# Cross-attention: running maximum taken one step later, and 8 of 15 probability tiles multiplied as high and low parts

## The reference

```python
# latents [4, 256, 512], context [4, 1601, 512], 32 query heads, 8 key/value heads of 128
kv = jnp.concatenate([context, latents], axis=1)
q = rms_norm((latents @ Wq) in 32 heads, q_norm_w)
k = rms_norm((kv @ Wk) in 8 heads, k_norm_w)
v = (kv @ Wv) in 8 heads
scores = jnp.einsum('bhgqd,bhkd->bhgqk', qg, k) / sqrt(128)
probs = softmax(scores, axis=-1)
out = jnp.einsum('bhgqk,bhkd->bhgqd', probs, v)
return out.reshape(...) @ Wo
```

## Time and profile before

| | |
|---|---|
| median of 3 runs | 3105.89 us (3101.67 to 3109.8) |
| the profiled execution | 3108.48 us |
| its span in the trace | 3106.6 us |
| PE busy, from 340 to 2930 us | 2586.37 of 2590 us |
| POOL busy in the same stretch | 1559.72 us |

### The profile page before, as it was taken

How to read it: one execution, slowest core, us unless ns; L and a number is a source line. 1 busy time by engine, 2 the same in 40 slices (tenths; PEclk the granted TensorE clock), 3 DMA queues, 4 the chain that set the end, 5 groups by cost and what they waited for, 6 DMA issues and landing times. The chain is left out here.

```text
span 3106.6 us, 43885 instructions
## 1 busy us (share of the span) xinstructions
PE 2868.3 (92%) x14348; PEld 2136.8 (69%) x14348; DVE 2117.3 (68%) x3447; ACT 1776.2 (57%) x3228; POOL 1740.6 (56%) x1729
## 2 busy tenths in 40 slices
PE   2239999999999999999999999999999999999976
PEld 1127777777777777777777777777777777777644
DVE  6726677777777777777777777776776767676654
ACT  1015666666666666666666666666666666665541
POOL 4413556566565565656656556565665655655550
PEclk7659999999999999999999999999999999999985
DMA  0075343343433434334433433433433333333201
GB/s 34 27 243 191 116 134 127 125 140 127 134 124 127 138 123 136 125 127 138 136 120 129 140 126 123 136 122 128 143 114 108 125 109 104 114 109 103 68 7 65
DMA packets 155728, 370.12 MB, mean 119 GB/s; under 512 B 12777, under 2 KB 46571, under 8 KB 155504
## 3 DMA queue, kind: packets, MB, share of 16 engines
q1 hardware_dynamic: 153752, 365.49, 35.7%
q10 hardware_dynamic: 1752, 1.84, 0.2%
HBM read 329.53 MB, written 37.75 MB: 118 GB/s over the span
## 5 line engine op out<-in xcount | busy, mean ns | idle before, releaser
L664 POOL TENSOR_TENSOR acc<-acc,scores 128x512 f32<-128x512 f32 (+1 forms) x832 | 1068.2, 1284 | 652.0 <-ACT scores L915 628.5
L1078 DVE SCALAR_TENSOR_TENSOR running_max<-S_ps,rk,running_max 128x512 f32<-128x512 f32 (+1 forms) x896 | 672.2, 750 | 710.8 <-ACT scores L907 705.1
L915 ACT ACTIVATE scores<-scores 128x512 f32<-128x512 f32 (+1 forms) x960 | 605.0, 631 | 933.8 <-DVE scores L1062 933.3
L749 PE MATMUL OT_ps<-scores,V 128*128 128x512 f32 (+1 forms) x1920 | 987.6, 597 | 9.6 <-issue 3.0
L720 PE MATMUL S_ps<-QT_hi,KT_hi 128*128 128x512 f32 (+1 forms) x960 | 732.1, 763 | 9.4 <-DVE running_max L1078 6.8
L1062 DVE TENSOR_TENSOR scores<-scores,Mb_ps 128x512 f32<-128x512 f32 (+1 forms) x960 | 649.8, 678 | 35.3 <-PE Mb_ps L832 32.1
L907 ACT ACTIVATE scores<-S_ps,rk 128x512 f32<-128x512 f32 (+1 forms) x960 | 646.8, 674 | 22.6 <-PE S_ps L722 22.3
L720 PE MATMUL K_ps<-Wkv_hi,kvT 128*128 128x256 f32 (+1 forms) x1664 | 469.6, 282 | 1.7 <-DVE V L1111 1.0
L722 PE MATMUL K_ps<-Wkv_hi,kvT 128*128 128x256 f32 (+1 forms) x1664 | 470.0, 282 | 0.0
L721 PE MATMUL K_ps<-Wkv_lo,kvT 128*128 128x256 f32 (+1 forms) x1664 | 469.4, 282 | 0.0
L722 PE MATMUL S_ps<-QT_hi,KT_lo 128*128 128x512 f32 (+1 forms) x960 | 378.9, 395 | 0.0
(11 more groups left out here) (177 smaller groups left out, 3909.7 us busy)
## 6 DMA issues: line engine op xcount, KB each, us to landing
kvT<-kvT_scratch SPq DMA_DIRECT2D x416, 512.0 KB, 3.3
w_stage<-in_L_xattn_Wq SPq DMA_DIRECT2D x64, 512.0 KB, 4.4
w_stage<-in_L_xattn_Wo SPq DMA_DIRECT2D x64, 512.0 KB, 4.4
kvT_scratch<-built SPq DMA_DIRECT2D x60, 512.0 KB, 2.9
xrow<-in_ctx SPq DMA_DIRECT2D x48, 256.0 KB
w_stage<-in_L_xattn_Wk SPq DMA_DIRECT2D x32, 256.0 KB, 3.0
w_stage<-in_L_xattn_Wv SPq DMA_DIRECT2D x32, 256.0 KB, 3.3
xT<-kvT_scratch SPq DMA_DIRECT2D x8, 512.0 KB, 5.3
```

The costliest lines, as they stand in the source:

```text
L664: e.tensor_tensor(a[0:r, :], a[0:r, :], prob(t)[0:r, :], ALU.add).then_inc(s_acc, 1)
L749: ins = e.matmul(OT_ps[:], V[v % 2][0:r, j, :], row[t % RING][0:r, :], start=first, stop=last)
L915: e.activation(d, d, ACT.Exp).then_inc(s_p, 1)
L1078: e.scalar_tensor_tensor(a, src, k, a, ALU.mult, ALU.max).then_inc(s_top, 1)
```

## The change

A tile j in `HALF` = 0, 1, 4, 5, 8, 9, 12, 13 is now multiplied as high and low parts: ACT takes the exponential twice, once rounded to fp32r into `P_hi` and once in fp32 into `P_sb` (two buffers of each), POOL subtracts them into `P_lo` (two buffers), and PE makes three fp32r products with `V_hi` and `V_lo`. The values of these tiles are split by ACT (`V_hi`) and DVE (`V_lo`) where DVE copied them before. The other 7 tiles (`FULL`) go as before. `pv` of such a tile waits for `P_lo`. On DVE `raise_max` of step s moves behind `shift` of step s+1, and in step c = 5 job X comes ahead of MT.

```diff
-            5: [("MT", 2 * v - 2), ("X", b + 1, 2 * h)],
+            5: [("X", b + 1, 2 * h), ("MT", 2 * v - 2)],
...
+            def lo(t):
+                j = t % NJ
+                if j in FULL:
+                    return
+                r = rows_of(j)
+                n = half_no(t)
+                e.wait_ge(s_p, t + 1)
+                if n >= 2:
+
+                    e.wait_ge(s_pv, half_tile(n - 2) + 1)
+                e.tensor_tensor(P_lo[n % 2][0:r, :], P_sb[n % 2][0:r, :], f(P_hi[n % 2][0:r, :]), ALU.subtract)\
+                    .then_inc(s_lo, 1)
...
                 if 0 <= s - WAIT < NS:
+                    lo(s - WAIT)
                     add(s - WAIT)
...
-                e.wait_ge(s_p, t + 1)
-                ins = e.matmul(OT_ps[:], V[v % 2][0:r, j, :], row[t % RING][0:r, :], start=first, stop=last)
+                if j in FULL:
+                    e.wait_ge(s_p, t + 1)
+                    ins = e.matmul(OT_ps[:], V_full[v % 2][0:r, FULL.index(j), :], row[t % RING][0:r, :],
+                                   start=first, stop=last)
+                else:
+                    i, n = HALF.index(j), half_no(t)
+                    e.wait_ge(s_lo, n + 1)
+                    ins = three(OT_ps[:], V_hi[v % 2][0:r, i, :], V_lo[v % 2][0:r, i, :],
+                                P_hi[n % 2][0:r, :], P_lo[n % 2][0:r, :], first, last)
...
-                e.activation(d, d, ACT.Exp).then_inc(s_p, 1)
+                if j in HALF:
+                    n = half_no(t)
+                    if n >= 2:
+
+                        old = half_tile(n - 2)
+                        e.wait_ge(s_pv, old + 1)
+                        e.wait_ge(s_acc, acc_no(old + 1 if old % NJ == 0 else old))
+                    e.activation(P_hi[n % 2][0:r, :], d, ACT.Exp)
+                e.activation(prob(t)[0:r, :], d, ACT.Exp).then_inc(s_p, 1)
...
+                if q in HALF_PAIRS:
+                    i = HALF.index(js[0])
+                    if v >= 2:
+
+                        e.wait_ge(s_pv, NJ * (2 * v - 3) + js[-1] + 1)
+                    e.activation(V_hi[v % 2][0:r, i:i + k, :], src[0:r, 0:k, HD:2 * HD], ACT.Copy).then_inc(s_vh, 1)
...
+                if q in HALF_PAIRS:
+                    e.wait_ge(s_vh, half_pair_no(v, q) + 1)
+                    at = slice(HALF.index(js[0]), HALF.index(js[0]) + k)
+                    e.tensor_tensor(V_lo[v % 2][0:r, at, :], src[0:r, 0:k, HD:2 * HD], f(V_hi[v % 2][0:r, at, :]),
+                                    ALU.subtract).then_inc(s_kr, 1)
...
                 if 0 <= s - WAIT < NS:
                     shift(s - WAIT)
+                if 0 <= s - 1 < NS:
+                    raise_max(s - 1)
...
                 for v, q in pairs(s - 1):
-                    copy_values(v, q)
-                if 0 <= s < NS:
-                    raise_max(s)
+                    low_values(v, q)
```

More of the change, by code:

```diff
@@ L317, in cross_attention @@
     LAST = (UNITS + 2) * CYCLE - AHEAD
+    FULL = [2, 3, 6, 7, 10, 11, 14]
+    HALF = [j for j in range(NJ) if j not in FULL]
     EPS = 1e-6
@@ L417, in acc_no, with half_no, half_tile @@
         return (NJ - 1) * p + j
+    def half_no(t):
+        p, j = divmod(t, NJ)
+        return len(HALF) * p + HALF.index(j)
+    def half_tile(n):
+        p, i = divmod(n, len(HALF))
+        return NJ * p + HALF[i]
     with ExitStack() as ctx:
@@ L432, in cross_attention @@
         KT_lo = sb("KT_lo", [P, NKP], F32R)
-        V = [sb(f"V{i}", [P, NJ, HD]) for i in range(2)]
+        V_hi = [sb(f"V_hi{i}", [P, len(HALF), HD], F32R) for i in range(2)]
+        V_lo = [sb(f"V_lo{i}", [P, len(HALF), HD], F32R) for i in range(2)]
+        V_full = [sb(f"V_full{i}", [P, len(FULL), HD]) for i in range(2)]
         QT_hi = [sb(f"QT_hi{i}", [P, QW], F32R) for i in range(2)]
@@ L436, in cross_attention @@
         row = [sb(f"scores{i}", [P, QW]) for i in range(RING)]
+        P_sb = [sb(f"P32_{i}", [P, QW]) for i in range(2)]
+        P_hi = [sb(f"P_hi{i}", [P, QW], F32R) for i in range(2)]
+        P_lo = [sb(f"P_lo{i}", [P, QW], F32R) for i in range(2)]
         Wkv_hi = [sb(f"Wkv_hi{i}", [P, C, 2 * HD], F32R) for i in range(2)]
@@ L491, in cross_attention @@
         s_p = sem("probabilities")
+        s_lo = sem("probabilities_lo")
         s_acc = sem("probabilities_added")
@@ L506, in cross_attention @@
         s_kc = sem("K_rows_copied")
+        s_vh = sem("V_hi_copied")
         s_sq = sem("squares")
@@ L523, in prob, with half_pair_no @@
         def prob(t):
-            return row[t % RING]
+            return row[t % RING] if t % NJ in FULL else P_sb[half_no(t) % 2]
+        FULL_PAIRS = [q for q in range(8) if 2 * q in FULL]
+        HALF_PAIRS = [q for q in range(8) if 2 * q in HALF]
+        def half_pair_no(v, q):
+            return len(HALF_PAIRS) * v + HALF_PAIRS.index(q)
         @block.sync
@@ L904, in copy_scores @@
                     t = s - RING
-                    e.wait_ge(s_pv, t + 1)
-                    e.wait_ge(s_acc, acc_no(t + 1 if t % NJ == 0 else t))
+                    if t % NJ in HALF:
+                        e.wait_ge(s_p, t + 1)
+                    else:
+                        e.wait_ge(s_pv, t + 1)
+                        e.wait_ge(s_acc, acc_no(t + 1 if t % NJ == 0 else t))
                 e.activation(row[s % RING][0:r, :], S_ps[s % 2][0:r, :], ACT.Copy, scale=rk[0:r, v % 2, j:j + 1])\
@@ L1101, in normalise, with low_values @@
                     e.tensor_tensor(natq[t][:], natq[t][:], factor, ALU.mult).then_inc(s_nat, 1)
-            def copy_values(v, q):
+            def low_values(v, q):
                 js = range(2 * q, min(2 * q + 2, NJ))
@@ L1106, in copy_values @@
                 src = K_ps[K_AT["P", v, q] % 2][:].rearrange("p (k n) -> p k n", n=2 * HD)
[L1107 to L1111, removed]
+                if q in HALF_PAIRS:
[3 more added lines that the diff above has]
+                                    ALU.subtract).then_inc(s_kr, 1)
+                else:
+                    e.wait_ge(s_kc, pair_no(v, q) + 1)
+                    at = slice(FULL.index(js[0]), FULL.index(js[0]) + k)
+                    if v >= 2:
+                        e.wait_ge(s_pv, NJ * (2 * v - 3) + js[-1] + 1)
+                    e.tensor_copy(V_full[v % 2][0:r, at, :], src[0:r, 0:k, HD:2 * HD]).then_inc(s_kr, 1)
             def drain(job):
```

## The result

The changed kernel takes 3008.27 us (median of 4 runs, 3007.19 to 3012.83) against 3106.4 us for the kernel before (4 runs, 3101.67 to 3109.8): ratio 0.9685, interval [0.9672, 0.9699]. That is 98 us less. The forecast was 74.5 less, and the time lies under its range of 3012 to 3062. The profiled execution's span is 3006.5 us, 100.1 less than before.

A forecast was written before the change was run, and what follows sets the result against it. The prediction took PE's own work to bound the stretch from 340 to 2930 us. 79.5 (PE) - 9 (stall) + 4 (end) = 74.5 us less than the median 3105.9 gave 3031 us, range 3012 to 3062.

The forecast's parts named there:

- The ring: Maximum, shift, exponential and copy across DVE and ACT, 2.62 us a turn; the later maximum cuts it, nothing charged.
- One of the forecast's signs: Between 340 and 2850 us, PE stays as good as full and 30 steps take 83.5 to 84 us.
- The start: The part up to 340 us, with few tiles: no gain taken.
- The end: From the scores of step 940 to POOL's last sum: becomes POOL's, 4 us less, between 0 and 9.6.
- PE, 79.5 us: In the full stretch, three fp32r products replace one fp32 product: 0.165 us less for each of 482 tiles.
- The stall at tile 17: PE waits for POOL's late P_lo at c = 19: 0.3 us a unit, 0 to 0.6, 9 us in all.
- A: Rival: all hidden, no stall at tile 17 and the whole 9.6 us gained at the end: 3017 us, 14%.
- B: Rival: POOL sets the pace in places, stalls of 0.8 to 1.1 us a unit, no end gain: 3056 to 3075, 16%.
- C: Rival: slower than before, POOL as the bound, from a P_lo of 2.0 us on; 3298 us at 2.39, 4%.
- D: Rival: on PE, three fp32r products cost as much as the fp32 tile, first weight load exposed: 3103 us, 3%.

The follow-up runs named there:

- e1: The kernel before with only the maximum of step s moved behind the shift of step s+1, all products in fp32: 3062.88 us, ratio 0.9861.
- e9: The kernel before with ACT's copy of OT_ps into OT_n put ahead of the exponential of the same step, maximum not moved: 3089.98 us, ratio 0.9942.
- e4: The changed kernel with P_lo left at zero and never computed, PE waiting for the exponential only; leaves out part of the computation: 2984.77 us, ratio 0.9607.
- e3: The changed kernel with the Newton group of nrm_a one step later on POOL, behind tile 17's P_lo and sum: 2997.06 us, ratio 0.9648.
- e5: e3 with the 16 changed tiles of the last unit multiplied in plain fp32 as before: 2983.91 us, ratio 0.9609.
- e8: e3 with the product of P_hi and V_lo left out, two products for each changed tile; leaves out part of the computation: 2888.08 us.
- e6: The changed kernel with every P_lo computed twice on POOL, the second behind the first: 3478.57 us (one run).
- e2: The changed kernel with the maximum back at its old place ahead of the next shift, so the split alone: 3369.48 us, ratio 1.0851.

## Why the prediction was wrong

The forecast was 79.5 - 9 in the stretch, 4 at the end and 0 at the start, and the time fell by 79.3, 8.2 (the rest's 0.5 with it) and 12.6. So 8.8 us are missing in the stretch (13.6 of the ring, less 4.5 by which the stall is larger and 0.3 of PE), 12.6 at the start and 4.2 at the end.

**The ring, "I charge nothing".** This step failed. It held for the ring with the split, where the new order covers it, but the sum also took the ring before as free, as if cutting it could give nothing back. The sentence behind it was "So in this stretch the time is PE's own work", read from PE busy 2586.37 of 2590 us. Those 27 waits of 0.36 us are hardly in that number. The product that comes after the wait is shown with 1.12 us in place of 1.02, and the ends of matmuls are modelled, so that a hole is partly covered by the instruction ahead of it: above, the hole that is left runs from 1373.07 to 1373.19, 0.12 us. From 500 to 2800 us such holes are all of the time that PE is not shown busy, 27 of them, 3.25 us together, each at c = 25 (counted in the trace). The list of waits had them. In e1 a step c = 25 is 0.38 us shorter; all in all the stretch gave back 13.6 us in e1 and 12.8 in e9.

One of the forecast's signs, 83.5 to 84 us for 30 steps, is met by the median unit (83.73), and that is luck. The 86.0 us it starts from is a mean, and some units are shorter than most. As means over tiles 60 to 940, 30 steps take 86.12 us before (2526.1 x 30/880) and 83.41 after, which is below the sign, as the ring's wait went too.

**The start, "I take nothing".** This term failed too. Measured 10.8 less from tile 0 to 60, 8.7 of them by the later maximum alone, and of these 2.9 come back with the OT_n copy alone (e9). For the rest, the waits of PE's loads from 250 to 400 us, before:

```profile
PEld S_ps L720 <- DVE running_max L1078: 8.9, 15, 1.9
```

PE has few jobs there, a step is about as short as the ring's turn of 2.62 us, and PE waits for the maximum. It is the same limit that I had seen behind 2930 us and had not looked for ahead of 340. The wait is 4.4 us in e1 and 2.6 after the change. The other 1.8 of the 12.6 us lie ahead of tile 0, where kernels that change nothing there differ by up to 5.

**The end, 4 us less, 0 to 9.6.** Measured 7.7 less, within its bounds. From the scores of step 940 to POOL's last sum I had forecast 79 us of POOL work for 88.6 of time (the count behind it is 20 lows and 36 sums; its "46 sums and lows' worth" is a slip). It is 80.9: 81.3 from the start of the product at 2840.4 in the table to the end of the row below, less its own 0.4. POOL is busy 77.97 us of it.

```profile
2920.42 1.26 POOL L700 TENSOR_TENSOR acc<-acc,scores 65x512 f32<-65x512 f32 x1
```

Two larger things stand behind the small sum: the ring gave back 21.9 (e1), the split took 14.2 (after against e1). 11.0 of these come back without the lows (e4 against e3), 11.7 without the split in the last unit (e5 against e3); the other 2.5 to 3 stay open.

While PE waited for the ring its granted clock fell as well. Over the 19 steps from tile 940 to 959 it was 0.90 before, and 1.00 in e1 and after the change; from 330 to 340 us it was 0.83 before and 1.00 in the other two. How much of what the ring gave back at the start and the end is clock, no run separates.

**PE, 79.5 us.** Right. e1 to e3 is this term with neither ring nor stall: 2512.5 - 2433.3 = 79.2 us, 2.67 us a unit and 0.167 a tile. One thing beside it wants setting right: the section of the Trainium skill that the prediction names (TensorE: Matmul & The Clock Gate, "Back-to-back issue gap") has the formula, 216 ns for 512 columns, as the gap of an isolated matmul, and about 131 ns for a stream of loads and matmuls; the 216 for matmuls back to back stand in the page's section "Wait — 56ns, not 53.3ns?". The trace's 232 and e8's 229 ns for fp32r lie above both.

**The stall at tile 17, 9 us, 0 to 18.** Right in place, in cause and within its bounds: 13.5 us (e3), 0.46 us a unit for 0.3. The rule of the Trainium skill that stood beside it (SBUF — State Buffer, "Who interferes with whom"), that a DVE instruction with two SBUF inputs and a GpSimd one that reads SBUF exclude each other, agrees with the rows: `OT_lo` 1.51 us for 0.68, and POOL's sum 1.76 for 1.29. I took a stall of half the worst case; with the whole 0.47 us in the count `P_lo` ends at 10.72 against 10.34, a stall of 0.38.

Worked out again with what was measured: 45.9 (the ring, in the span) + 79.2 - 13.5 - 14.2 = 97.4 us, and 2.6 for what is left of the 100.0: 2.1 less at the start by the split, and 0.5 in the first and the last column.

**Rivals.** A had the whole 9.6 us of the end and no stall; the time 3017 was the nearest, but its reason is refuted, since the stall is there. B: POOL sets the pace in places, true of c = 19 and of the end, not at its price. C: POOL's `P_lo` is 1.318 us and not 2.0; e6, with two lows in a row, shows POOL as the bound. D: the three products save their 0.167 us a tile (e1 to e3), and only the one at c = 19 waits for `P_lo` in the stretch.

**The two halves of the change don't add up.** The later maximum alone gives 43 us, the split alone takes 264, both together give 98. With the ring cut first, the split is worth 55; with the ring in place it is the worst thing here.

## What to carry to other kernels

Where one engine is shown full, still read the list of its waits for short ones that come once a unit, and price the stages in which it is not full each on its own: a ring through two other engines sets the pace exactly there. Cut a ring before adding work to an engine inside it, and count all that stands in it at its worst step, not only the pair of instructions that is always there. For a result that goes through a shared in-order queue, add up that queue from its last wait to this result against the time at which it is wanted; here that gave the stall to 0.2 us, and moving five short instructions behind it took it away.

## What the runs showed of the hardware

- The lock between DVE and POOL moves with the order: before, it made `rk` 0.67 us for 0.20; now it makes `OT_lo` 1.51 for 0.68 and the sum 1.76 for 1.29. It lasted as long in e3 (1.76) and cost nothing there, since PE was not waiting for what stood behind it.
- ACT's instructions follow each other closer than their durations: from the `P_hi` exponential to the next one 0.54 us for 0.63, and to the copy 0.52 for 0.62 (the ring's turn in e2).
- With PE waiting for POOL at many steps (e6) the granted clock of a 1000 us window fell from 1.00, the 2.4 GHz level, to a mean of 0.97; in the end of the changed kernel, with PE busy 15.73 of 25 us, the mean was 0.80, partly at the 1.2 GHz level. In the kernel before it was 0.90 from tile 940 to 959, with PE busy 40.6 of 52.1 us.
- A short wait of a full PE hardly shows in its busy time: 0.36 us of waiting left a hole of 0.12 in the rows and cost 0.38 in the step.
